# A recurrent scan block: GpSimd's four LayerNorm operations at four steps instead of one

## The chip, the cores and the metric

The kernel runs on one core of a Trainium2 chip. The metric is the device time of one execution in microseconds; lower is better. Engines are named TensorE (PE in the profile), VectorE (DVE), ScalarE (ACT), GpSimd (POOL) and SyncE (SP).

## What is computed

The input has 32 sequences ("rows" below, 0 to 31) of 512 tokens with 256 channels. Per row:

```
xn  = (x - mean(x)) / sqrt(var(x) + 1e-5)            # LayerNorm over the 256 channels
s   = scan_forward(xn) + reverse(scan_backward(reverse(xn)))
g   = silu(xn + 0.3 * expert_ffn(xn))                # one of 8 experts per row, exact GELU inside
out = x + s * g

# each scan, 16 states per channel and direction:
delta, B, C = project(xn);  delta = softplus(delta @ W + b)
h[t] = exp(delta[t] * A) * h[t-1] + delta[t] * B[t] * xn[t]
y[t] = sum over states of C[t] * h[t]  +  D * xn[t]
```

## The kernel before

**Stages.** A prologue prepares weights and row 0. Then every row is a loop over 32 steps `s`, one for each state (16 forward, 16 backward). In a step:
- a decay, exp(delta * A), is made by ScalarE (`make_decay`), two steps ahead or more;
- the input term bx = dx * B is made by GpSimd for 18 of the 32 states (`times_b`, the states in `POOL_B`: 0 to 4, 7, 10, 12, 16 to 21, 23, 25, 27, 31), and for the other 14 by ScalarE (`scale_dx`) and TensorE (transposes);
- VectorE runs the recurrence over the 512 tokens and 2 x 128 channels (`scan`, L868, tile hs);
- hs is multiplied by C, on GpSimd for the 15 states in `POOL_C` (2, 4, 5, 7, 9 to 12, 16, 18, 20, 22, 24, 26, 27), four steps after their own (`C_LAG = 4`), on VectorE for the others (both write hc);
- TensorE sums the hc in PSUM (`add_state`).

Large operations of GpSimd are all 128 x 1024 in float32. Below, "bx 4", "hc 27" and "scan 31" are these operations for states 4, 27 and 31.

**What runs ahead.** While row r is scanned, the "front" of row r + 1 is done in the same 32 steps: tables of step numbers at the top of the kernel say at which step an engine issues which piece. For LayerNorm:
- step 0 (`MEAN`), VectorE: `mean_variance`, after scan 0 of row r: `bn_stats` and `bn_aggr` (L808, L811) give mv;
- step 1 (`SCALE`), ScalarE: `normalise_scale` (L547 to L553): lnv = ln(var + eps), nvar, nmean, rs = exp(-0.5 lnv), rsq = rs squared;
- step 6 (`SHIFT`), GpSimd: `shift_of`, one Newton step on rs: nwt = rsq * nvar, nwt = nwt + 1.5, rs = nwt * rs, shift = nmean * rs, each on 128 x 4 elements and each waiting for the one before;
- step 6 (`NORM`), ScalarE: `normalise` writes xn.

**What sets the order.** Nothing is scheduled by a tool: every engine issues its instructions in the order of the code, and an instruction whose semaphore hasn't been reached holds those behind it on its engine. In a step GpSimd issues, in this order, `times_b`, `times_c`, the rest of this row's front, the next row's front, and `residual` of the row before at step 4 (its og). An lg (`log1p`, second direction of the row being scanned) also stands at step 4.

**Buffers.** bx has 4 slots (`RING`), hs 4 (`HSLOTS`), hc 4. `scan` of state s writes slot s % 4 of hs, and so waits until hc of state s - 4 has been made, by GpSimd's count `s_hcp` where that state is in `POOL_C`:

```python
used = s - HSLOTS
if used % STEPS in POOL_C:
    wait(dve, s_hcp, (row if used >= 0 else row - 1) * NPC + on_pool(used % STEPS) + 1)
```

In ScalarE's loop body of step 31 stand: the decay of state 1 of the next row (it waits for scan 31 of this row), the second copy dxT, SiLU, GELU and the table load behind them; of step 0: the decay of state 2; of step 1: the decay of state 3, `scale_dx` and `normalise_scale`.

Of the kernel before, what the change touches and what calls it, by code (L numbers as in the profile page):

```python
# [5 lines left out]
def mamba_moe_block(nc, x, xw_f, dtw_f, dtb_f, alog_f, d_f, xw_b, dtw_b, dtb_b, alog_b, d_b,  # L6
# [12 lines left out]
    ALU, ACT = mybir.AluOpType, mybir.ActivationFunctionType  # L19
# [4 lines left out]
    C = T // P  # L24
    N = alog_f.shape[1]
    R = dtw_f.shape[1]
    NE, _, F = w1.shape
    FT = F // P
    STEPS = 2 * N
# [4 lines left out]
    BRING, CRING, C_AHEAD = 6, 5, 3  # L34
    TSLOTS, XSLOTS = 3, 3

    MEAN, SCALE, SHIFT, NORM = 0, 1, 6, 6
    TRANS, XNT, PROJECT, HIGH, LOW = (6, 7), (8, 9), (8, 9), 11, 12
    B_TURN, B_COPY = 11, 13
    EXPAND, ABS = (14, 15, 24, 25), (16, 17, 26, 27)  # L40
# [28 lines left out]
    with ctx:  # L69
        def sb(name, shape, dt=f32):  # L70
            return ctx.enter_context(nc.sbuf_tensor(name, shape, dt))
# [4 lines left out]
        def sem(name):  # L76
            return ctx.enter_context(nc.semaphore(name))
# [47 lines left out]
        rs = sb("rs", [P, C])  # L125
        nvar = sb("nvar", [P, C])
        nmean = sb("nmean", [P, C])
        rsq = sb("rsq", [P, C])
        nwt = sb("nwt", [P, C])
        half_eps = sb("half_eps", [P, 1])  # L130
        shift = sb("shift", [P, C])
# [57 lines left out]
        s_bn, s_mv, s_ln, s_rs, s_shift = (sem(n) for n in ("bn_done", "mv_done", "ln_done", "rs_done", "shift_done"))  # L189
        s_xn, s_xnT = sem("xn_done"), sem("xnT_done")  # L190
# [6 lines left out]
        s_sqr = sem("newton_operands")  # L197
        s_nwt, s_xnwt = sem("newton_steps"), sem("router_newton_steps")
# [15 lines left out]
        def wait(eng, s, value):  # L214

            if not isinstance(value, int) or value > 0:
                eng.wait_ge(s, value)  # L217

        def wait_alone(eng, s, value):

            if not isinstance(value, int) or value > 0:
                eng.wait_ge(s, value)
                eng.sem_inc(s_passed, 1)
# [205 lines left out]
        def _(pool):  # L429
# [13 lines left out]
            def step_x(row, par, g):  # L443
                pool.wait_ge(s_delta, row * 2 + g + 1)
                pool.wait_ge(s_xnT, row * 2 + 2)

                wait(pool, s_dxturn, (row - 1) * 2 * DT + g * DT + DT)
                nc.gpsimd.tensor_tensor(dx[:, g, :, :], delta[:, g * (1 + par), :, :], xnT[:, par, :, :], ALU.mult).then_inc(s_dx, 1)  # L448

            def cut(row, par, g):  # L450

                pool.wait_ge(s_dx, row * 2 + g + 1)
                later, edge = (1, 0) if g == 0 else (0, T - 1)
                nc.gpsimd.memset(delta[:, g * (1 + par), later, edge:edge + 1], NO_CARRY).then_inc(s_cut, 1)

            def log1p(row, g):
                pool.wait_ge(s_ratio, row * 2 + g + 1)
                nc.gpsimd.tensor_tensor(lg[:, :, :], lg[:, :, :], ex[:, g, :, :], ALU.mult).then_inc(s_log1p, 1)  # L458

            def step_size(row, par, g):  # L460
                pool.wait_ge(s_log1p, row * 2 + g + 1)
                pool.wait_ge(s_relu, row * 4 + 2 * g + 2)
                nc.gpsimd.tensor_tensor(delta[:, g * (1 + par), :, :], lg[:, :, :], delta[:, g * (1 + par), :, :], ALU.add).then_inc(s_delta, 1)  # L463
# [23 lines left out]
            def residual(row):  # L487
                pool.wait_ge(s_yg, row + 1)
                pool.wait_ge(s_xr, row * 16 + 16)
                nc.gpsimd.tensor_tensor(og[:, :, :], og[:, :, :], xres[:, :, :], ALU.add).then_inc(s_out, 1)  # L490

            def shift_of(row):

                wait_alone(pool, s_sqr, row * 3 + 3)
                wait(pool, s_xn, row * C)
                G = nc.gpsimd
                G.tensor_tensor(nwt[:, :], rsq[:, :], nvar[:, :], ALU.mult).then_inc(s_nwt, 1)
                wait_alone(pool, s_nwt, row * 3 + 1)
                G.tensor_scalar(nwt[:, :], nwt[:, :], 1.5, None, ALU.add).then_inc(s_nwt, 1)
                pool.wait_ge(s_nwt, row * 3 + 2)  # L500
                G.tensor_tensor(rs[:, :], nwt[:, :], rs[:, :], ALU.mult).then_inc(s_nwt, 1)
                pool.wait_ge(s_nwt, row * 3 + 3)
                G.tensor_tensor(shift[:, :], nmean[:, :], rs[:, :], ALU.mult).then_inc(s_shift, 1)

            def front(row, par, s):
                if s == SHIFT:
                    shift_of(row)
                if s in LOG1P:
                    log1p(row, LOG1P.index(s))
                if s in STEPSIZE:  # L510
                    step_size(row, par, STEPSIZE.index(s))
                if s in DX:
                    step_x(row, par, DX.index(s))
                if s in CUT:
                    cut(row, par, CUT.index(s))

            shift_of(0)
            log1p(0, 0)
            step_size(0, 0, 0)
# [3 lines left out]
            def body(row, par, last):  # L523
                for s in range(STEPS):
                    if s in POOL_B:
                        times_b(row, s)
                    if s - C_LAG in POOL_C:
                        times_c(row, s - C_LAG)
                    front(row, par, s + STEPS)
                    if not last:  # L530
                        front(row + 1, 1 - par, s)
                    if s == Y_RESIDUAL and not (isinstance(row, int) and row == 0):
                        residual(row - 1)
# [723 lines left out]
```

## Time and profile before

| | |
|---|---|
| median of 3 runs | 3113.33 us (3111.51 to 3114.2) |
| profiled execution | 3109.25 us |
| its span, first to last instruction | 3107.4 us |
| busy, GpSimd / VectorE / ScalarE / TensorE | 3013.3 / 3021.9 / 2940.2 / 2481.6 us |
| GpSimd's large operations, bx (576) and hc (480) | 1360.9 and 1133.6 us busy |
| VectorE's scans (576 and 448) | 1310.2 and 1005.6 us busy |
| mean granted TensorE clock | 0.961 of full speed |

"Busy" is the time in which an instruction of the engine is under way. The profile gives each instruction's start and duration; on GpSimd and VectorE neighbouring instructions overlap slightly, so the distance from one start to the next tells better what an instruction costs its engine than its duration. Idle time is what passed on an engine between two instructions, and the releaser is the instruction that ended it.

### The profile page before, as it was taken

What the parts mean: (1) busy time and instruction counts of PE and PEld (TensorE: products, weight loads), DVE (VectorE), ACT (ScalarE), POOL (GpSimd) and SP (SyncE); (2) the same over time, 40 slices, a digit from 0 to 9 for tenths busy, and PEclk for the clock granted to TensorE, in tenths of its full rate; (3) what the DMA queues carried; (4) which work ended last, traced back from release to release, by engine and by line L of the source; (5) the groups of instructions that cost most, each with busy time, mean ns of one, the idle gap of its engine ahead of it and who ended that gap; (6) DMA issues with size and microseconds to landing.
All of it is one profiled execution on the core that took longest, in us unless ns stands there. A gap on an engine that the chain in (4) does not pass through costs nothing. (4 is left out here: it accounts for less than half of the span.)

```text
span 3107.4 us, 49213 instructions
## 1 busy us (share of the span) xinstructions
PE 2481.6 (80%) x15990; PEld 1965.3 (63%) x15990; DVE 3021.9 (97%) x1995; ACT 2940.2 (95%) x5242; POOL 3013.3 (97%) x1486
## 2 busy tenths in 40 slices
PE   8788877888878878778888788787788787887886
PEld 6666666666656666666666566666666666666665
DVE  4999999999999999999999999999999999999999
ACT  6899999999999999999999999999999999999995
POOL 3999999999999999999999999999999999999997
PEclk9999999999999999999999999999999999999998
DMA  6443334443334443344443344433444433444341
GB/s 208 121 141 125 125 108 130 141 134 117 122 122 129 143 125 122 114 127 139 134 125 123 113 131 144 128 116 121 122 140 136 125 122 109 131 144 131 108 122 55
DMA packets 258004, 394.17 MB, mean 127 GB/s; under 512 B 45003, under 2 KB 99028, under 8 KB 257748
## 3 DMA queue, kind: packets, MB, share of 16 engines
q1 hardware_dynamic: 257748, 391.03, 41.4%
q8 instruction: 127, 2.08, 0.3%
q14 instruction: 129, 1.06, 0.1%
HBM read 348.98 MB, written 25.18 MB: 120 GB/s over the span
## 5 line engine op out<-in xcount | busy, mean ns | idle before, releaser
L483 POOL TENSOR_TENSOR bx<-dx,b_sb 128x1024 f32<-128x1024 f32 x576 | 1360.9, 2383 | 0.9 <-PE y L1105 0.8
L868 DVE TENSOR_TENSOR_SCAN hs<-decay,bx 128x1024 f32<-128x1024 f32 x576 | 1310.2, 2279 | 15.4 <-POOL bx L483 5.3
L471 POOL TENSOR_TENSOR hc<-hs,c_sb 128x1024 f32<-128x1024 f32 x480 | 1133.6, 2371 | 22.7 <-DVE hs L868 21.0
L1105 PE MATMUL y<-ident,hc 128*128 128x128 f32 x8192 | 1068.3, 277 | 36.2 <-DVE hc L847 36.2
L1105 PEld LDWEIGHTS y<-ident,hc 128*128 128x128 f32 x8192 | 941.9, 143 | 148.7 <-DVE hc L847 106.2
L868 DVE TENSOR_TENSOR_SCAN hs<-decay_sb,decay 128x1024 f32<-128x1024 f32 x448 | 1005.6, 2268 | 11.7 <-issue 10.4
L685 ACT ACTIVATE decay<-delta,rate 128x512 f32<-128x512 f32 x1152 | 745.7, 684 | 41.1 <-DVE hs L868 36.6
L597 ACT ACTIVATE dxb<-dxT,btok 128x256 f32<-128x256 f32 x1792 | 759.2, 503 | 0.4 <-PE decay L1078 0.3
L1078 PE MATMUL decay<-ident,dxb 128*128 128x128 f32 x3584 | 477.2, 276 | 246.0 <-DVE hs L868 212.5
L847 DVE TENSOR_TENSOR hc<-hs,c 128x1024 f32<-128x1024 f32 x544 | 651.0, 1197 | 6.2 <-PE c L1086 5.5
L1078 PEld LDWEIGHTS decay<-ident,dxb 128*128 128x128 f32 x3584 | 396.5, 141 | 402.5 <-issue 258.9
L685 ACT ACTIVATE decay_sb<-delta,rate 128x512 f32<-128x512 f32 x896 | 588.8, 716 | 0.1
L1086 PE MATMUL c<-dbc,selector 128*128 128x512 f32 x544 | 271.3, 499 | 203.0 <-DVE hc L847 203.0
L1047 PE MATMUL front<-w2o_sb,hT 128*128 128x256 f32 x1024 | 297.3, 442 | 39.1 <-issue 39.1
L1031 PE MATMUL front<-xnT,w_sb 128*128 128x512 f32 x512 | 244.3, 599 | 41.6 <-ACT delta L610 41.5
L1047 PEld LDWEIGHTS front<-w2o_sb,hT 128*128 128x128 f32 x1024 | 218.0, 224 | 79.9 <-issue 48.2
L1086 PEld LDWEIGHTS c<-dbc,selector 128*128 128x128 f32 x544 | 105.7, 194 | 256.0 <-DVE hc L847 248.4
L458 POOL TENSOR_TENSOR lg<-lg,ex 128x1024 f32<-128x1024 f32 x64 | 152.0, 2375 | 29.3 <-ACT lg L627 29.0
L1031 PEld LDWEIGHTS front<-xnT,w_sb 128*128 128x128 f32 x512 | 87.3, 190 | 116.8 <-issue 61.2
L463 POOL TENSOR_TENSOR delta<-lg,delta 128x1024 f32<-128x1024 f32 x64 | 152.3, 2380 | 0.1
L448 POOL TENSOR_TENSOR dx<-delta,xnT 128x1024 f32<-128x1024 f32 x64 | 151.7, 2370 | 0.1
L587 ACT ACTIVATE dxT<-front 128x512 f32<-128x512 f32 x128 | 75.1, 587 | 33.6 <-PE front L1007 33.6
(128 smaller groups left out, 2037.6 us busy)
## 6 DMA issues: line engine op xcount, KB each, us to landing
b_sb<-b_scratch SPq DMA_DIRECT2D x576, 256.0 KB, 3.3
c_sb<-b_scratch SPq DMA_DIRECT2D x480, 256.0 KB, 3.6
xin<-in_L_attn_x_dram SPq DMA_DIRECT2D x32, 512.0 KB, 6.3
w_sb<-in_L_ffn_W_dram SPq DMA_DIRECT2D x32, 512.0 KB, 3.4
w2o_sb<-w2o_scratch SPq DMA_DIRECT2D x32, 512.0 KB
xres<-in_L_attn_x_dram SPq DMA_DIRECT2D x32, 512.0 KB, 5.4
out_dram<-og SPq DMA_DIRECT2D x32, 512.0 KB, 4.3
dbc<-high SPq DMA_DIRECT2D x64, 128.0 KB, 2.3
```

The source lines that it names most:

```text
L463: nc.gpsimd.tensor_tensor(delta[:, g * (1 + par), :, :], lg[:, :, :], delta[:, g * (1 + par), :, :], ALU.add).then_inc(s_delta, 1)
L471: nc.gpsimd.tensor_tensor(hc[:, s % RING, :, :], hs[:, s % HSLOTS, :, :], c_sb[:, i % CRING, :].unsqueeze(1).broadcast_to([P, DT, T]), ALU ...
L483: nc.gpsimd.tensor_tensor(bx[:, i % RING, :, :], dx[:, g, :, :], b_sb[:, i % BRING, :].unsqueeze(1).broadcast_to([P, DT, T]), ALU.mult).th ...
L597: A(dxb[:, (row * NT + i) % XSLOTS, c, :], dxT[:, g, c, :], ACT.Copy, scale=btok[:, par, c, g, n:n + 1]).then_inc(s_dxb, 1)
L685: return A(to[:, k, :], delta[:, g * (1 + par), k, :], ACT.Exp, scale=rate[:, g, k, n:n + 1])
L847: V.tensor_tensor(hc[:, s % RING, :, :], hs[:, s % HSLOTS, :, :], cps[:, :].unsqueeze(1).broadcast_to([P, DT, T]), ALU.mult).then_inc(s_hc, 1)
L868: V.tensor_tensor_scan(hs[:, s % HSLOTS, :, :].rearrange("p k t -> p (k t)")[:, u], factor.rearrange("p k t -> p (k t)")[:, u], data.rearr ...
L1031: ins = M(fps[:, :], w1_sb[:, k, j * P:(j + 1) * P], xnT[:, par, k, :], start=(k == 0), stop=(k == DT - 1))
L1047: M(to, hT[:, j, c * P:(c + 1) * P], w2o_sb[:, j, :], start=(j == 0), stop=False)
L1078: ins = nc.tensor.transpose(dps[s % DSLOTS][:, k, c * P:(c + 1) * P], dxb[:, (row * NT + i) % XSLOTS, c, k * P:(k + 1) * P], ident[:, :])
L1086: M(cps[:, :], selector[:, N + n:N + n + 1].broadcast_to([P, P]), dbc[:, par, g, :], start=True, stop=True).then_inc(s_cps, 1)
L1105: ins = M(yps[:, c, k * P:(k + 1) * P], hc[:, s % RING, k, c * P:(c + 1) * P], ident[:, :], start=False, stop=(s == ADDED[-1]), is_transpo ...
```

## The change

GpSimd's `shift_of` is split into four functions. The product is issued at step 3 of the row before, the sum with 1.5 at step 4, the new rs at step 5 and shift at step 6. The product waits for ScalarE's three operands; the wait for the xn of the row before, which protects rs and shift from being overwritten too early, now stands at rs. In the prologue the four are called one behind the other. Nothing else is changed.

```diff
--- before.py
+++ after.py
@@ -34,7 +34,7 @@
     BRING, CRING, C_AHEAD = 6, 5, 3
     TSLOTS, XSLOTS = 3, 3
 
-    MEAN, SCALE, SHIFT, NORM = 0, 1, 6, 6
+    MEAN, SCALE, SHIFT, NORM = 0, 1, (3, 4, 5, 6), 6
     TRANS, XNT, PROJECT, HIGH, LOW = (6, 7), (8, 9), (8, 9), 11, 12
     B_TURN, B_COPY = 11, 13
     EXPAND, ABS = (14, 15, 24, 25), (16, 17, 26, 27)
@@ -489,21 +489,32 @@
                 pool.wait_ge(s_xr, row * 16 + 16)
                 nc.gpsimd.tensor_tensor(og[:, :, :], og[:, :, :], xres[:, :, :], ALU.add).then_inc(s_out, 1)
 
+            def newton_product(row):
+
+                pool.wait_ge(s_sqr, row * 3 + 3)
+                nc.gpsimd.tensor_tensor(nwt[:, :], rsq[:, :], nvar[:, :], ALU.mult).then_inc(s_nwt, 1)
+
+            def newton_sum(row):
+                pool.wait_ge(s_nwt, row * 3 + 1)
+                nc.gpsimd.tensor_scalar(nwt[:, :], nwt[:, :], 1.5, None, ALU.add).then_inc(s_nwt, 1)
+
+            def newton_deviation(row):
+                pool.wait_ge(s_nwt, row * 3 + 2)
+                wait(pool, s_xn, row * C)
+                nc.gpsimd.tensor_tensor(rs[:, :], nwt[:, :], rs[:, :], ALU.mult).then_inc(s_nwt, 1)
+
             def shift_of(row):
-
-                wait_alone(pool, s_sqr, row * 3 + 3)
-                wait(pool, s_xn, row * C)
-                G = nc.gpsimd
-                G.tensor_tensor(nwt[:, :], rsq[:, :], nvar[:, :], ALU.mult).then_inc(s_nwt, 1)
-                wait_alone(pool, s_nwt, row * 3 + 1)
-                G.tensor_scalar(nwt[:, :], nwt[:, :], 1.5, None, ALU.add).then_inc(s_nwt, 1)
-                pool.wait_ge(s_nwt, row * 3 + 2)
-                G.tensor_tensor(rs[:, :], nwt[:, :], rs[:, :], ALU.mult).then_inc(s_nwt, 1)
                 pool.wait_ge(s_nwt, row * 3 + 3)
-                G.tensor_tensor(shift[:, :], nmean[:, :], rs[:, :], ALU.mult).then_inc(s_shift, 1)
+                nc.gpsimd.tensor_tensor(shift[:, :], nmean[:, :], rs[:, :], ALU.mult).then_inc(s_shift, 1)
 
             def front(row, par, s):
-                if s == SHIFT:
+                if s == SHIFT[0]:
+                    newton_product(row)
+                if s == SHIFT[1]:
+                    newton_sum(row)
+                if s == SHIFT[2]:
+                    newton_deviation(row)
+                if s == SHIFT[3]:
                     shift_of(row)
                 if s in LOG1P:
                     log1p(row, LOG1P.index(s))
@@ -514,6 +525,9 @@
                 if s in CUT:
                     cut(row, par, CUT.index(s))
 
+            newton_product(0)
+            newton_sum(0)
+            newton_deviation(0)
             shift_of(0)
             log1p(0, 0)
             step_size(0, 0, 0)
```

GpSimd's queue from step 3 on of any row but the first and last (nwt and rs, shift are the four operations; bx, hc, lg and og are large ones). Before:

```order
L483 TENSOR_TENSOR bx<-dx,b_sb 128x1024 [waits scan_done,b_loaded3]
L483 TENSOR_TENSOR bx<-dx,b_sb 128x1024 [waits scan_done,b_loaded4]
L458 TENSOR_TENSOR lg<-lg,ex 128x1024 [waits ratio_done]
L490 TENSOR_TENSOR og<-og,xres 128x1024 [waits xres_loaded,yg_done]
L471 TENSOR_TENSOR hc<-hs,c_sb 128x1024 [waits sum_states_done,c_loaded0,scan_done]
L497 TENSOR_TENSOR nwt<-rsq,nvar 128x4 [waits newton_operands,xn_done]
L499 TENSOR_SCALAR nwt<-nwt 128x4 [waits newton_steps]
L501 TENSOR_TENSOR rs<-nwt,rs 128x4 [waits newton_steps]
L503 TENSOR_TENSOR shift<-nmean,rs 128x4 [waits newton_steps]
L483 TENSOR_TENSOR bx<-dx,b_sb 128x1024 [waits scan_done,b_loaded5]
```

The same place in the changed kernel:

```order
L483 TENSOR_TENSOR bx<-dx,b_sb 128x1024 [waits scan_done,b_loaded3]
L495 TENSOR_TENSOR nwt<-rsq,nvar 128x4 [waits newton_operands]
L483 TENSOR_TENSOR bx<-dx,b_sb 128x1024 [waits scan_done,b_loaded4]
L458 TENSOR_TENSOR lg<-lg,ex 128x1024 [waits ratio_done]
L499 TENSOR_SCALAR nwt<-nwt 128x4 [waits newton_steps]
L490 TENSOR_TENSOR og<-og,xres 128x1024 [waits xres_loaded,yg_done]
L504 TENSOR_TENSOR rs<-nwt,rs 128x4 [waits xn_done,newton_steps]
L471 TENSOR_TENSOR hc<-hs,c_sb 128x1024 [waits sum_states_done,c_loaded0,scan_done]
L508 TENSOR_TENSOR shift<-nmean,rs 128x4 [waits newton_steps]
L483 TENSOR_TENSOR bx<-dx,b_sb 128x1024 [waits scan_done,b_loaded5]
```

The product, which waits for ScalarE's "newton_operands", was behind bx 4, lg, og and hc 2 and is now ahead of them; the other three stand one large operation apart, and shift has its place ahead of bx 7.

The same steps in row 0, on GpSimd, where there is no og of a row before. Before:

```order
L483 TENSOR_TENSOR bx<-dx,b_sb 128x1024 [waits b_loaded3]
L483 TENSOR_TENSOR bx<-dx,b_sb 128x1024 [waits scan_done,b_loaded4]
L458 TENSOR_TENSOR lg<-lg,ex 128x1024 [waits ratio_done]
L471 TENSOR_TENSOR hc<-hs,c_sb 128x1024 [waits c_loaded0,scan_done]
L497 TENSOR_TENSOR nwt<-rsq,nvar 128x4 [waits newton_operands,xn_done]
L499 TENSOR_SCALAR nwt<-nwt 128x4 [waits newton_steps]
L501 TENSOR_TENSOR rs<-nwt,rs 128x4 [waits newton_steps]
L503 TENSOR_TENSOR shift<-nmean,rs 128x4 [waits newton_steps]
L483 TENSOR_TENSOR bx<-dx,b_sb 128x1024 [waits scan_done,b_loaded5]
```

and in the changed kernel:

```order
L483 TENSOR_TENSOR bx<-dx,b_sb 128x1024 [waits b_loaded3]
L495 TENSOR_TENSOR nwt<-rsq,nvar 128x4 [waits newton_operands]
L483 TENSOR_TENSOR bx<-dx,b_sb 128x1024 [waits scan_done,b_loaded4]
L458 TENSOR_TENSOR lg<-lg,ex 128x1024 [waits ratio_done]
L499 TENSOR_SCALAR nwt<-nwt 128x4 [waits newton_steps]
L504 TENSOR_TENSOR rs<-nwt,rs 128x4 [waits xn_done,newton_steps]
L471 TENSOR_TENSOR hc<-hs,c_sb 128x1024 [waits c_loaded0,scan_done]
L508 TENSOR_TENSOR shift<-nmean,rs 128x4 [waits newton_steps]
L483 TENSOR_TENSOR bx<-dx,b_sb 128x1024 [waits scan_done,b_loaded5]
```

Here the product moved ahead of bx 4, lg and hc 2. No instruction moved on another engine.

## Rows read from the trace of the kernel before

**Rows 1.** The page, part 1: busy us (share of the span) x instructions
```profile
PE 2481.6 (80%) x15990; PEld 1965.3 (63%) x15990; DVE 3021.9 (97%) x1995; ACT 2940.2 (95%) x5242; POOL 3013.3 (97%) x1486
```

**Rows 2.** Lines, GpSimd, whole span: out<-in xcount | busy us, mean ns | idle before
```profile
L497 POOL TENSOR_TENSOR nwt<-rsq,nvar 128x4 f32<-128x4 f32 x32 | 6.6, 206 | 11.2 <-ACT rsq L553 11.2
```

**Rows 3.** Timeline, GpSimd, row 12: start us, us, instruction, [idle before <-releaser]
```profile
1200.10 11.66 POOL L483 TENSOR_TENSOR bx<-dx,b_sb 128x1024 f32<-128x1024 f32 x5
1211.73 2.35 POOL L458 TENSOR_TENSOR lg<-lg,ex 128x1024 f32<-128x1024 f32 x1
...
1218.68 0.20 POOL L497 TENSOR_TENSOR nwt<-rsq,nvar 128x4 f32<-128x4 f32 x1
1219.07 0.22 POOL L499 TENSOR_SCALAR nwt<-nwt 128x4 f32<-128x4 f32 x1 [0.20 <-POOL nwt L497]
...
1219.65 0.20 POOL L503 TENSOR_TENSOR shift<-nmean,rs 128x4 f32<-128x4 f32 x1
1219.81 2.38 POOL L483 TENSOR_TENSOR bx<-dx,b_sb 128x1024 f32<-128x1024 f32 x1
```

**Rows 4.** Timeline, ScalarE, row 12
```profile
1203.43 1.30 ACT L685 ACTIVATE decay<-delta,rate 128x512 f32<-128x512 f32 x2 [0.18 <-DVE hs L868]
1204.68 0.58 ACT L587 ACTIVATE dxT<-front 128x512 f32<-128x512 f32 x1
...
1216.91 0.20 ACT L553 ACTIVATE rsq<-rs 128x4 f32<-128x4 f32 x1
...
1228.56 2.06 ACT L560 ACTIVATE xn<-xin,shift,rs 128x256 f32<-128x256 f32 x4
```

**Rows 5.** Timeline, VectorE, start of row 12
```profile
1201.06 2.28 DVE L868 TENSOR_TENSOR_SCAN hs<-decay,bx 128x1024 f32<-128x1024 f32 x1
...
1204.37 2.28 DVE L868 TENSOR_TENSOR_SCAN hs<-decay,bx 128x1024 f32<-128x1024 f32 x1
...
1209.22 0.38 DVE L811 BATCH_NORM_AGGREGATE mv<-stats 128x2 f32<-128x6 f32 x4
```

**Rows 6.** Timeline, GpSimd, end of row 12 (hc 24, hc 27, next bx 0)
```profile
1282.74 2.35 POOL L471 TENSOR_TENSOR hc<-hs,c_sb 128x1024 f32<-128x1024 f32 x1
...
1292.26 2.38 POOL L471 TENSOR_TENSOR hc<-hs,c_sb 128x1024 f32<-128x1024 f32 x1
1294.61 2.37 POOL L483 TENSOR_TENSOR bx<-dx,b_sb 128x1024 f32<-128x1024 f32 x1
```

**Rows 7.** Timeline, VectorE, end of row 12 (scans 28 and 29, 31, 0)
```profile
1286.65 4.44 DVE L868 TENSOR_TENSOR_SCAN hs<-decay_sb,decay 128x1024 f32<-128x1024 f32 x2
...
1295.43 2.28 DVE L868 TENSOR_TENSOR_SCAN hs<-decay,bx 128x1024 f32<-128x1024 f32 x1
...
1298.74 2.28 DVE L868 TENSOR_TENSOR_SCAN hs<-decay,bx 128x1024 f32<-128x1024 f32 x1
```

**Rows 8.** Timeline, GpSimd, row 0
```profile
44.99 11.64 POOL L483 TENSOR_TENSOR bx<-dx,b_sb 128x1024 f32<-128x1024 f32 x5
...
73.09 0.20 POOL L497 TENSOR_TENSOR nwt<-rsq,nvar 128x4 f32<-128x4 f32 x1 [5.96 <-ACT rsq L553]
```

**Rows 9.** Timeline, ScalarE, row 0
```profile
72.71 0.21 ACT L553 ACTIVATE rsq<-rs 128x4 f32<-128x4 f32 x1
```

**Rows 10.** Timeline, VectorE: scan 4 of row 0, scan 0 of rows 1 and 31
```profile
74.19 2.29 DVE L868 TENSOR_TENSOR_SCAN hs<-decay,bx 128x1024 f32<-128x1024 f32 x1 [0.56 <-issue]
...
161.40 2.29 DVE L868 TENSOR_TENSOR_SCAN hs<-decay,bx 128x1024 f32<-128x1024 f32 x1
...
3004.39 2.29 DVE L868 TENSOR_TENSOR_SCAN hs<-decay,bx 128x1024 f32<-128x1024 f32 x1
```

**Rows 11.** Windows: us; busy us of each engine; PEclk, DMA share, GB/s
```profile
1210.00:1216.00 6.00, 5.06 (x16) 3.63 (x17) 6.00 (x4) 5.97 (x10) 6.00 (x3) 0.57 0.56 175
```

**Rows 12.** Timeline, TensorE, before ScalarE's copy at 1204.68
```profile
1201.54 1.91 PE L1105 MATMUL y<-ident,hc 128*128 128x128 f32 x16
1203.28 0.60 PE L1007 MATMUL front<-ident,dx 128*128 128x128 f32 x4
```

## The prediction

> **What bounds the kernel now.** I read the page first: GpSimd is busy 97% of the span, VectorE 97%, ScalarE 95% [rows 1]. With three engines so full, whichever waits loses, so I read one row in the timelines (row 12; "S" is the start of its scan of state 0, 1204.37 [rows 5]). GpSimd: its large operations start every 2.32 us, back to back; the only place without one is the Newton chain, which holds the engine from 1218.68 to the start of the next bx at 1219.81, 1.13 us for four operations of 0.2 us [rows 3]. VectorE: from this S to the next, 1298.74, are 94.37 us [rows 7]. The mean over rows 1 to 31 is (3004.39 - 161.40) / 30 = 94.77 us [rows 10]. GpSimd and VectorE thus run in step, about evenly full.
>
> Next I asked where the chain's input comes from. Its first product needs rsq, the fifth of ScalarE's small activations. ScalarE waits 0.18 us for VectorE's scan of state 31 (started 1201.06 [rows 5], the wait stands at 1203.43 [rows 4]) and from there works through its queue: two decays, a copy, SiLU and GELU with their table loads, four decays, four scalings, then the small ones for LayerNorm up to rsq, which ends at 1216.91 + 0.20 = 1217.11 [rows 4]. The statistics themselves were there at 1209.22 + 0.38 = 1209.60 [rows 5]: what is late is ScalarE's turn, not the data. So rsq is ready 16.05 us after the start of scan 31, or S + 12.74. Today the product starts at 1218.68, 1.57 us later, and over all 32 rows it waited only 11.2 us, mostly in the first two [rows 2].
>
> **The change, part by part.**
>
> *Product moved from step 6 to step 3.* On GpSimd it now stands ahead of bx of state 4. Five bx take from 1200.10 to the lg at 1211.73, so bx 4 starts at 1211.73 - 2.32 = 1209.41 [rows 3]. The product would stand there, and its input comes at 1217.11: a wait of 7.7 us. GpSimd works in order, so bx 4, lg, og, hc, bx 7 and all that follows wait too. Nothing covers this: GpSimd has no spare time [rows 1]. The question is only how much of it comes back through slack.
>
> *The three others* find their inputs done (each follows its predecessor by a large operation). Apart, each costs what lies between the start of shift and the next start, 19.81 - 19.65 = 0.16 us [rows 3]. Bounds: 0.05 and 0.3 us (0.3 is the spacing inside the chain; below, an operation hidden by its large neighbours). I take 0.16, the same kind of operation beside the same kind. Four cost 0.64 instead of 1.13: 0.5 us saved per row, range 0 to 1.
>
> *How much slack is there?* If GpSimd falls behind VectorE, who waits first? VectorE's scan of state s overwrites the hs slot of state s - 4 and so waits for GpSimd's hc of it. hc of state 27 ends at 1292.26 + 2.38 = 1294.64 [rows 6], scan 31 starts 1295.43 [rows 7]: 0.79 us of slack. hc 24 ends 1285.09, scan 28 starts 1286.65: 1.56. The next row's bx 0 ends at 1294.61 + 2.37 = 1296.98, its scan 0 starts 1298.74: 1.76 [rows 6, 7]. A wait of 7.7 us cannot be stored in 0.79, and it is not paid once either: ScalarE is released by scan 31, so when scan 31 waits for GpSimd, rsq is later by the same amount. That closes a loop, and its length is the new period of a row:
> - start of scan 31 to end of rsq: 16.05 [rows 4, 5]
> - release of the product by rsq: in the first row rsq ends at 72.92 and the product starts at 73.09 after waiting: 0.17 [rows 8, 9]
> - product 0.16; bx 4, lg, og, hc: 1218.68 - 1209.41 = 9.27; the other three small ones 3 x 0.16 = 0.48 [rows 3]
> - from bx 7 (1219.81) to the end of hc 27 (1294.64), unchanged work: 74.83 [rows 3, 6]
> - release of scan 31: 0.04 (nothing shows it for this pair; between 0.02 and the 0.18 of ScalarE's wait above).
>
> Sum 101.00 us, against 94.77: +6.23 per row. This is the wait of 7.7 less the 0.5 saved and the 0.79 of slack, roughly. There are 30 such periods (rows 1 to 30; row 31 has no next row to normalise, and its 103 us to the end stay as they are). 30 x 6.23 = 187 us.
>
> *First row.* Its bx 3 ends at about 54.3 (five bx from 44.99), and the product waits until 73.09 for the rsq it waits for already [rows 8]. bx 4 then ends at 73.25 + 2.36 = 75.6, and scan 4, which started at 74.19, needs it [rows 10]: +1.4 us. Beyond that GpSimd waits for VectorE in this row anyway.
>
> *Prologue, SP queue, PE.* In the prologue the four calls keep their order and nothing lies between them: 0. GpSimd issues no DMA; the SP queue's loads of b and c wait for GpSimd's counts and move with it, several loads ahead: 0. ScalarE's normalising of xn needs shift. With the terms above shift starts at 12.74 + 0.17 + 0.16 + 9.27 + 0.32 = S + 22.66 and ends 0.2 later; xn starts at 1228.56, S + 24.19 [rows 4]: 0. PE's additions of GpSimd's hc come later, but the scans and their own hc, which PE adds too, come later by nearly as much: 0, with the 1 us that eight additions take (16 in 1.91 [rows 12]) as the upper bound per row.
>
> **Sum.** 187 + 1.4 = 188. The profiled execution took 3109.25 us (span 3107.40): 3109.25 + 188 = 3297.6. The median of the runs stands 4.1 us above that execution, so 3301. With the bounds (small operations 0.4 to 0.5 us either way per row, releases 0.2, PE up to 1 us more) the case itself reaches from 3280 to 3335.
>
> **A rule that says the opposite.** In the rows, GpSimd and VectorE are both at 97% [rows 1] and the product's wait decides. The Trainium skill, "Perfetto Trace Analysis", section "Identifying the Most-Contended Engine", says to take the engine with the highest occupancy as the bound and to optimise it first. By that rule the sum would be the saving alone. That rule's case is the first rival below.
>
> **Rivals.**
> 1. *Faster: the wait doesn't happen, or happens once.* GpSimd loses only the chain's latency: 31 x 0.5 = 15 us, 3098. It needs rsq before GpSimd is through with bx 3, 7.7 us earlier than today against GpSimd. It decides at 0.5 us: a shorter wait than that is a gain. Against it: ScalarE's unbroken queue from scan 31 to rsq, and only 0.79 us of slack at scan 31. The Trainium skill's rule of the most-contended engine points to this time. Chance 0.02; a balance near zero 0.02 more.
> 2. *Slower, but less.* If scan 31 isn't what holds VectorE but scan 0 is (bx 0 ends 2.34 us after hc 27, while scan 0 starts 3.31 us after scan 31), up to 0.97 us per row is not paid, and ScalarE gains as much on its queue while VectorE waits: up to 2 us per row, 3241 to 3272. Against: hs has four slots and the code's wait names hc 27. Chance 0.06.
> 3. *Slower still.* ScalarE's stretch gets longer. It holds a copy that PE feeds, and PE's granted clock is not always full: 0.57 of 1.00 between 1210 and 1216, so the lower of its two levels (1.2 and 2.4 GHz) for most of it [rows 11]. If PE, now more idle, gets it elsewhere, the 16 additions (1.9 us) and 4 transposes (0.6) ahead of this copy take twice their time, less the 0.8 us between the transposes' end and the copy [rows 4, 12]: 1.7 us more per row, with what stands ahead of them about 2: 3361. Chance 0.10.
>
> **How the numbers follow.** The forecast case has 0.80, predicted time 3301. The range takes it whole and the nearer parts of rivals 2 and 3: 3262 to 3345. Within 0.2% (6 us) is what a measurement of this kernel can't tell from no change. Faster 0.02, same 0.02, slower 0.96.
>
> **What the new profile should show.** GpSimd's product with some 7 us of idle time ahead of it in each of 31 rows, released by rsq, in all near 210 to 240 us with the first row's 18.6; GpSimd's busy share down to about 91%. Rows of one length, 101.0 us. VectorE waiting for GpSimd at scans 28 and 31 and, before them, in the first half of the row, together 6.6 us per row. rsq still 16.05 us after the start of scan 31. I am wrong if the product's idle time is small, or if it is 7 us and the rows are nevertheless shorter than 99 us.

## The result, and the profile after

| | before | changed |
|---|---|---|
| median | 3113.76 us (4 runs) | 3304.11 us (4 runs, 3300.68 to 3304.54) |
| ratio, 95% interval | | 1.0611 [1.0599, 1.0624] |
| profiled execution / its span | 3109.25 / 3107.40 us | 3300.68 / 3298.9 us |
| mean length of rows 1 to 30 | 94.77 us | 101.13 us |
| mean granted TensorE clock | 0.961 | 0.917 |

The changed kernel is 190 us (6.1%) slower. The forecast was 3301 us in a range of 3262 to 3345.

The page of the changed kernel, span and part 1 (compare [rows 1]):

```profile
span 3298.9 us, 49180 instructions
...
PE 2612.7 (79%) x15990; PEld 2087.3 (63%) x15990; DVE 3042.6 (92%) x1995; ACT 2942.0 (89%) x5242; POOL 3008.7 (91%) x1486
```

All engines do the same work in a longer time. GpSimd's busy time is even 5 us less, though its share falls from 97% to 91%. The line of the product (columns as in [rows 2]) has the difference:

```profile
L495 POOL TENSOR_TENSOR nwt<-rsq,nvar 128x4 f32<-128x4 f32 x32 | 6.5, 203 | 238.0 <-ACT rsq L567 238.0
```

238.0 us of idle time stand ahead of the 32 products, against 11.2 before. 5.2 of the 238.0 us are the prologue's, in both kernels. The idle time ahead of GpSimd's hc, nearly all of it for VectorE, fell from 22.7 to 3.5 us meanwhile.

One row, row 12 again. GpSimd's timeline (compare [rows 3]):

```profile
1270.75 9.35 POOL L483 TENSOR_TENSOR bx<-dx,b_sb 128x1024 f32<-128x1024 f32 x4
1287.06 0.20 POOL L495 TENSOR_TENSOR nwt<-rsq,nvar 128x4 f32<-128x4 f32 x1 [6.96 <-ACT rsq L567]
1287.21 2.38 POOL L483 TENSOR_TENSOR bx<-dx,b_sb 128x1024 f32<-128x1024 f32 x1
1289.53 2.39 POOL L458 TENSOR_TENSOR lg<-lg,ex 128x1024 f32<-128x1024 f32 x1
1291.86 0.24 POOL L499 TENSOR_SCALAR nwt<-nwt 128x4 f32<-128x4 f32 x1
1292.05 2.39 POOL L490 TENSOR_TENSOR og<-og,xres 128x1024 f32<-128x1024 f32 x1
1294.38 0.22 POOL L504 TENSOR_TENSOR rs<-nwt,rs 128x4 f32<-128x4 f32 x1
1294.53 2.37 POOL L471 TENSOR_TENSOR hc<-hs,c_sb 128x1024 f32<-128x1024 f32 x1
1296.85 0.21 POOL L508 TENSOR_TENSOR shift<-nmean,rs 128x4 f32<-128x4 f32 x1
1297.01 2.38 POOL L483 TENSOR_TENSOR bx<-dx,b_sb 128x1024 f32<-128x1024 f32 x1
```

Four bx end at 1280.10, the product starts at 1287.06: 6.96 us of idle time, ended by rsq. Behind it everything is as dense as before. The other three find their inputs ready; from the start of shift to the next bx are 0.16 us, as before, and for the others it is 0.15 us (0.19 for the sum with 1.5): from product to bx 7 are 9.95 us, four large operations and four small ones.

ScalarE (compare [rows 4]) and VectorE at the start of the same row (compare [rows 5]; scan 31, then scan 0):

```profile
1273.30 1.30 ACT L699 ACTIVATE decay<-delta,rate 128x512 f32<-128x512 f32 x2 [0.55 <-DVE hs L882]
...
1286.78 0.21 ACT L567 ACTIVATE rsq<-rs 128x4 f32<-128x4 f32 x1
...
1300.00 2.08 ACT L574 ACTIVATE xn<-xin,shift,rs 128x256 f32<-128x256 f32 x4 [1.16 <-DVE zz L836]
```

```profile
1270.92 2.29 DVE L882 TENSOR_TENSOR_SCAN hs<-decay,bx 128x1024 f32<-128x1024 f32 x1 [0.63 <-POOL hc L471]
...
1274.24 2.28 DVE L882 TENSOR_TENSOR_SCAN hs<-decay,bx 128x1024 f32<-128x1024 f32 x1
```

rsq ends at 1286.99, 16.07 us after the start of scan 31 (1270.92); before, these were 16.05. And scan 31 itself now has idle time ahead of it, 0.63 us, ended by a GpSimd hc.

The end of the row, GpSimd's hc 24 and hc 27 (compare [rows 6]) and VectorE's scans 28, 31 and 0 (compare [rows 7]):

```profile
1359.86 2.40 POOL L471 TENSOR_TENSOR hc<-hs,c_sb 128x1024 f32<-128x1024 f32 x1
...
1369.46 2.36 POOL L471 TENSOR_TENSOR hc<-hs,c_sb 128x1024 f32<-128x1024 f32 x1
```

```profile
1362.40 4.46 DVE L882 TENSOR_TENSOR_SCAN hs<-decay_sb,decay 128x1024 f32<-128x1024 f32 x2 [1.25 <-ACT decay_sb L699]
...
1371.95 2.29 DVE L882 TENSOR_TENSOR_SCAN hs<-decay,bx 128x1024 f32<-128x1024 f32 x1 [0.66 <-POOL hc L471]
...
1375.27 2.28 DVE L882 TENSOR_TENSOR_SCAN hs<-decay,bx 128x1024 f32<-128x1024 f32 x1
```

hc 27 ends at 1371.82, scan 31 starts at 1371.95: the 0.79 us of slack are gone, and the loop is closed. Scan 28 waited 1.25 us; the profile names a decay of ScalarE as the last releaser, but by ScalarE's timeline this decay had been done some 12 us earlier, and hc 24 ended at 1359.86 + 2.40 = 1362.26, 0.14 us ahead of the scan. That is one of the cases in which the named releaser isn't the one that held. VectorE's own list of waits shows the sums that carry GpSimd's name (us in total, times, longest):

```profile
DVE hs L882 <- POOL hc L471: 117.0, 128, 1.9
DVE hs L882 <- POOL bx L483: 48.0, 32, 5.3
```

### The profile page after: what moved, and what is told of

Read it like the earlier page. It is cut to its first block, busy times and chain, and to the rows that moved or that the text cites. A ratio compares the mean times of both kernels' runs of the same rounds, so it can differ in the third digit from the quotient of the medians.

```text
span 3298.9 us, 49180 instructions
## 1 busy us (share of the span) xinstructions
PE 2612.7 (79%) x15990; PEld 2087.3 (63%) x15990; DVE 3042.6 (92%) x1995; ACT 2942.0 (89%) x5242; POOL 3008.7 (91%) x1486
## 4 chain that ended last, share of the span: by engine, by line
POOL 24%; PE 18%; issue 13%; ACT 11%; DVE 7%; DMA 1%; POOLq 0%; DVEq 0%; ACTq 0%; SPq 0%
POOL hc L471 10%; POOL bx L483 9%; PE y L1119 6%; PE front L1061 4%; DVE hs L882 4%; ACT decay L699 4%; ACT dxb L611 3%; DVE hc L861 3%; POOL delta L463 2%; PE decay L1092 2%; PE c L1100 2%; POOL dx L448 2%; ACT decay_sb L699 1%; PE y L1109 1%; POOL lg L458 1%
## 5 line engine op out<-in xcount | busy, mean ns | idle before, releaser
L1119 PE MATMUL y<-ident,hc 128*128 128x128 f32 x8192 | 1151.4, 291 | 84.0 <-POOL hc L471 43.3
L1119 PEld LDWEIGHTS y<-ident,hc 128*128 128x128 f32 x8192 | 1009.0, 150 | 213.1 <-DVE hc L861 104.9
L1092 PE MATMUL decay<-ident,dxb 128*128 128x128 f32 x3584 | 506.2, 287 | 300.7 <-DVE hs L882 241.2
L1092 PEld LDWEIGHTS decay<-ident,dxb 128*128 128x128 f32 x3584 | 422.5, 148 | 457.6 <-issue 269.7
L1100 PE MATMUL c<-dbc,selector 128*128 128x512 f32 x544 | 285.1, 524 | 162.2 <-DVE hc L861 162.2
L1100 PEld LDWEIGHTS c<-dbc,selector 128*128 128x128 f32 x544 | 112.4, 207 | 199.7 <-DVE hc L861 192.3
L495 POOL TENSOR_TENSOR nwt<-rsq,nvar 128x4 f32<-128x4 f32 x32 | 6.5, 203 | 238.0 <-ACT rsq L567 238.0
```

The source lines that it names most:

```text
L1092: ins = nc.tensor.transpose(dps[s % DSLOTS][:, k, c * P:(c + 1) * P], dxb[:, (row * NT + i) % XSLOTS, c, k * P:(k + 1) * P], ident[:, :])
L1100: M(cps[:, :], selector[:, N + n:N + n + 1].broadcast_to([P, P]), dbc[:, par, g, :], start=True, stop=True).then_inc(s_cps, 1)
L1119: ins = M(yps[:, c, k * P:(k + 1) * P], hc[:, s % RING, k, c * P:(c + 1) * P], ident[:, :], start=False, stop=(s == ADDED[-1]), is_transpo ...
```

## The experiments

The theory: a row's length is that of a closed loop, scan 31, ScalarE's queue up to rsq, the product's wait, GpSimd's work to hc 27, and scan 31 again. The rivals: small operations cost something by standing apart (1.5 us each would do); or the bound is another and the wait only goes along. In the arithmetic of the expectations, 3113 and 3304 are the medians of the two kernels. Every run's ratio is to the kernel before, run on the same chip.

**Where the product stands.** Three runs with the product alone at step 3, 4 and 5, the other three a chain at step 6:

```diff
-    MEAN, SCALE, SHIFT, NORM = 0, 1, (3, 4, 5, 6), 6
+    MEAN, SCALE, SHIFT, NORM = 0, 1, (3, 6, 6, 6), 6      # first run; then (4, 6, 6, 6) and (5, 6, 6, 6)
```

> Only the product stands at step 3; sum, rs and shift are a chain at step 6 again. Theory (the product's wait for rsq is all of it; the period of a row is the loop through that wait): the loop keeps its wait and pays 0.73 us for a chain of three in place of 3 x 0.16: 101.1 + 0.25 us per row, 3304 + 8 = 3312. Rival (the cost comes from small operations standing apart among large ones, 190 us over 4 x 31 operations, about 1.5 us each): only one of four stands apart, 3113 + 48 = 3161.

> Product at step 4 (behind bx 4 and lg, ahead of og), the other three a chain at step 6. Theory: two large operations (4.64 us) leave the part of the loop that lies behind the wait: 16.06 + 0.08 + 0.16 + 4.64 + 0.73 + 74.83 + 0.13 = 96.6 us per row against 94.77: 3113 + 56 = 3169, and the product waits some 2.5 us per row. Rival (cost per operation that stands apart): as with the product at step 3, 3161, and the wait doesn't set the time; by it this run and the one before are equal.

> Product at step 5 (behind og, ahead of hc 2), the other three a chain at step 6. Theory: the loop is 16.06 + 0.08 + 0.16 + 2.32 + 0.73 + 74.83 + 0.13 = 94.3 us, below the 94.4 to 94.8 that VectorE needs for a row, so it no longer sets the time although the product still waits (some 0.5 us or less per row): 3106 to 3120, no change that can be told. Rival (cost per operation apart): 3161.

Measured: 3309.29 us (1.063 [1.0612, 1.0648]), 3172.38 us (1.0191 [1.0174, 1.0208]) and 3112.78 us (1.000 [0.9991, 1.001]). The product's line in the three:

```profile
L495 POOL TENSOR_TENSOR nwt<-rsq,nvar 128x4 f32<-128x4 f32 x32 | 6.4, 201 | 236.8 <-ACT rsq L567 236.8
```

```profile
L495 POOL TENSOR_TENSOR nwt<-rsq,nvar 128x4 f32<-128x4 f32 x32 | 6.5, 203 | 95.3 <-ACT rsq L567 95.3
```

```profile
L495 POOL TENSOR_TENSOR nwt<-rsq,nvar 128x4 f32<-128x4 f32 x32 | 6.5, 203 | 33.0 <-ACT rsq L567 32.3
```

The rival is out: with one operation apart the loss is not a quarter but all of it and 5 us more, and it shrinks by 137 us when the same operation stands two large ones later. The theory's 3312, 3169 and 3106 to 3120 were met within 3.4 us. The third run says most about reading: there the product still waits, 33.0 us in all (5.2 in the prologue, 14.0 in the first row, 0.0 to 1.4 in each of the others), and the kernel isn't slower. The loop is only about 94.3 us long with this product, and what the product waits is what VectorE's row was longer than that: 0.01 us after a row of 94.38 us, 0.47 after one of 94.79, 0.85 after one of 95.16. From row 1 on, hc 27 still ends at least 0.15 us ahead of scan 31, so nothing of it reaches VectorE. In that kernel's row 12 the product stands directly between two large operations (GpSimd's timeline):

```profile
1219.48 0.20 POOL L495 TENSOR_TENSOR nwt<-rsq,nvar 128x4 f32<-128x4 f32 x1
1219.63 2.36 POOL L471 TENSOR_TENSOR hc<-hs,c_sb 128x1024 f32<-128x1024 f32 x1
1221.95 0.23 POOL L499 TENSOR_SCALAR nwt<-nwt 128x4 f32<-128x4 f32 x1
```

**The four places without the wait.**

```diff
-                pool.wait_ge(s_sqr, row * 3 + 3)
-                nc.gpsimd.tensor_tensor(nwt[:, :], rsq[:, :], nvar[:, :], ALU.mult).then_inc(s_nwt, 1)
+                if isinstance(row, int) and row == 0:
+                    pool.wait_ge(s_sqr, 3)
+                nc.gpsimd.tensor_tensor(nwt[:, :], ident[:, 0:C], ident[:, C:2 * C], ALU.mult).then_inc(s_nwt, 1)
...
-                nc.gpsimd.tensor_tensor(rs[:, :], nwt[:, :], rs[:, :], ALU.mult).then_inc(s_nwt, 1)
+                nc.gpsimd.tensor_tensor(rs2[:, :], nwt[:, :], ident[:, 0:C], ALU.mult).then_inc(s_nwt, 1)
...
-                nc.gpsimd.tensor_tensor(shift[:, :], nmean[:, :], rs[:, :], ALU.mult).then_inc(s_shift, 1)
+                nc.gpsimd.tensor_tensor(shift[:, :], ident[:, 0:C], rs2[:, :], ALU.mult).then_inc(s_shift, 1)
```

(The wait for ScalarE is left only in the prologue. And, since shift no longer follows ScalarE's operands, VectorE's `mean_variance` waits for these operands by their own count.)

> The four operations stand at steps 3, 4, 5 and 6 as in the changed kernel, but read only constants, so that none waits for ScalarE. Left out: the Newton step on rs, and shift has nothing to do with the mean (the sizes and counts of operations are the same). Theory (it is the wait alone): the loss is gone, 3098 to 3115. Rival (places or number of gaps cost by themselves): 3304 stays in large part, above 3200.

Measured: 3111.6 us, 0.9997 [0.9987, 1.0006]. The same four places, the same count and size of operations, no loss. Where they stand costs nothing; what the first of them waits for costs everything.

**Whose lateness it is.** The changed kernel with ScalarE's small operations one step earlier in its queue:

```diff
-    MEAN, SCALE, SHIFT, NORM = 0, 1, (3, 4, 5, 6), 6
+    MEAN, SCALE, SHIFT, NORM = 0, 0, (3, 4, 5, 6), 6
```

> The changed kernel with ScalarE's normalise_scale at step 0 in place of 1, that is ahead of one decay pair (1.25 us) and one group of four scalings (1.6 us). Theory (rsq is late because of ScalarE's turn, not its data): rsq comes 2.8 us sooner after the start of scan 31, the loop is 2.8 us shorter, 98.3 us per row: 3304 - 85 = 3219. Rival (rsq is bound by the statistics, or GpSimd's wait is with something else that comes at the same time): 3304 stays.

Measured: 3219.62 us, 1.0343 [1.0328, 1.0359]. The product's line:

```profile
L495 POOL TENSOR_TENSOR nwt<-rsq,nvar 128x4 f32<-128x4 f32 x32 | 6.4, 201 | 152.1 <-ACT rsq L567 152.1
```

The stall fell by 86 us and the time by 84. The statistics are made at the same place of VectorE's queue as before, so it was ScalarE's turn that was late, as [rows 4, 5] had it.

**Where GpSimd's lateness passes on.** The changed kernel with a fifth slot of hs, so that scan 31 waits for hc 26 and no longer for hc 27; for the room, b_sb has five slots instead of six, and a control has the latter alone:

```diff
-    HSLOTS = 4
-    BRING, CRING, C_AHEAD = 6, 5, 3
+    HSLOTS = 5
+    BRING, CRING, C_AHEAD = 5, 5, 3
```

(and the slot is `(row * STEPS + s) % HSLOTS`.)

> The changed kernel with five slots of hs in place of four, and five of b_sb in place of six for the room; the next run is its control. Scan 31 then waits for hc 26, done one large pair earlier, and bx 0 and scan 0 close the loop. Theory (scan 31's wait for hc 27 is the place where GpSimd's lateness passes to VectorE and from there to ScalarE): the loop loses 3.31 - 2.34 - 0.1, some 0.9 to 1.0 us, and up to 1.2 more where ScalarE gets ahead while VectorE waits at scan 0: 3238 to 3276. Rival (hs slots don't matter, the loop closes at scan 0 anyway): as the control.

> Control of the run before: the changed kernel with five slots of b_sb and four of hs. Theory: b arrives early enough either way, 3304. Rival (one slot less makes GpSimd wait for b): above 3315.

Measured: the control 3302.8 us, 1.0617 [1.0599, 1.0634], as the changed kernel; with five slots of hs 3278.53 us, 1.0537 [1.052, 1.0555]. 24 us less than the control: the direction and the place are as expected, the size is 2.5 us short of the range. VectorE now waits for bx, and its list of waits no longer names an hc of GpSimd (of the changed kernel's waits above, some 70% were for hc):

```profile
DVE hs L882 <- POOL bx L483: 131.0, 104, 6.2
```

Most rows are 99.8 us long, 1.2 less than the changed kernel's 101.0. But 5 of the 30 are 101.1 to 101.5. Ahead of such a row, this is ScalarE's queue behind scan 31 (which starts at 860.59), and TensorE's timeline ahead of the second copy:

```profile
862.97 1.30 ACT L699 ACTIVATE decay<-delta,rate 128x512 f32<-128x512 f32 x2 [0.28 <-DVE hs L882]
867.02 0.60 ACT L601 ACTIVATE dxT<-front 128x512 f32<-128x512 f32 x1 [2.74 <-PE front L1021]
```

```profile
862.92 3.31 PE L1119 MATMUL y<-ident,hc 128*128 128x128 f32 x15 [1.80 <-POOL hc L471]
```

TensorE adds the states in order. Its additions waited 1.80 us for GpSimd's hc 27, the transposes that feed ScalarE's second copy stood behind them, the copy had 2.74 us of idle time ahead of it, and rsq came 18.9 us after scan 31 in place of 16.07. But the wait for hc 27 alone doesn't make a row long. Behind the scan 31 at 2463.26 hc 27 is as late, and the additions wait nearly as long:

```profile
2465.58 1.97 PE L1119 MATMUL y<-ident,hc 128*128 128x128 f32 x16 [1.68 <-POOL hc L471]
```

There the copy waits 1.07 us, rsq comes 17.2 us after scan 31, and the next row is 99.7 us long. What sets the long rows apart is how long the 16 additions take: 3.52 us for all of them in the row above and 2.95 to 3.52 us in the five, against 1.97. The granted clock differs as much (windows in the two rows, columns as in [rows 11]):

```profile
863.00:866.00 3.00, 3.00 (x15) 3.00 (x16) 1.75 (x2) 1.27 (x2) 3.00 (x2) 0.52 0.03 10
2465.60:2467.50 1.90, 1.90 (x18) 1.90 (x19) 1.06 (x1) 1.30 (x2) 1.90 (x1) 1.00 0.09 26
```

In all five it is 0.52 to 0.63 during these additions, near the lower level. So two things together make ScalarE's stretch up to 2.9 us longer and undo VectorE's early scan 31: the additions start late, behind hc 27, and they run at the lower clock. The second is the third rival of the prediction. Without these five rows, which cost about 1.6 us each, the run would lie within the range; why the clock is lower there and not elsewhere isn't shown.

**Can the spreading be of use at all?** If the four stand apart where all inputs are there, GpSimd saves what the prediction counted. Two ways of placing them, and as a bound the kernel before without the Newton step:

```diff
-    MEAN, SCALE, SHIFT, NORM = 0, 1, (3, 4, 5, 6), 6
+    MEAN, SCALE, SHIFT, NORM = 0, 0, (5, 6, 7, 8), 6      # all apart; the other: 0, 1, (6, 6, 7, 8), 6
```

```diff
-                G.tensor_tensor(nwt[:, :], rsq[:, :], nvar[:, :], ALU.mult).then_inc(s_nwt, 1)
...
-                G.tensor_tensor(rs[:, :], nwt[:, :], rs[:, :], ALU.mult).then_inc(s_nwt, 1)
-                pool.wait_ge(s_nwt, row * 3 + 3)
```

> normalise_scale at step 0 and the four operations apart at steps 5, 6, 7 and 8, where every input is there in time. GpSimd saves about 0.5 us per row and waits for nothing. Theory (VectorE's own work, 94.4 us, sets the row once GpSimd doesn't wait): no change from before, 3106 to 3114. Rival (GpSimd sets it too, its saving comes through): 31 x 0.5 = 15 us, 3098.

> Product and sum at step 6, rs at 7, shift at 8, normalise_scale where it was. GpSimd saves about 0.3 us per row; no operation waits for ScalarE, and shift (about S + 22.7) is there before ScalarE's xn (S + 24.2). Theory: as before, 3106 to 3116. Rival (GpSimd sets the row): 3104; if shift came too late for xn, some tenths of a us more per row, 3120 to 3130.

> The kernel before with the three Newton operations left out: GpSimd makes only shift = nmean * rs from ScalarE's rs at step 6. Left out: the refinement of rs. GpSimd has 0.98 us less work per row, the most that any placing of these operations could save. Theory (VectorE sets the row): 3104 to 3114. Rival (GpSimd sets it): 31 x 0.98 = 30 us, 3083.

Measured: 3113.41 us (1.0002 [0.9993, 1.0011]), 3112.31 us (0.9999 [0.999, 1.0008]) and 3110.48 us (0.9994 [0.9985, 1.0003]). None differs from the kernel before, not even the last, from which 1 us of GpSimd's work per row was taken. In the first two, GpSimd's saving went into slack: from row 1 on, hc 27 ends at least 1.2 us ahead of scan 31, where before it was 0.5 us at the least. The page of the last:

```profile
span 3109.3 us, 49085 instructions
...
PE 2483.4 (80%) x15990; PEld 1966.9 (63%) x15990; DVE 3021.5 (97%) x1995; ACT 2940.9 (95%) x5242; POOL 2997.4 (96%) x1390
```

GpSimd's busy time is 16 us less than in [rows 1], VectorE's is the same within 1 us and the span within 2. About half of its rows are 94.37 to 94.39 us long, as in the kernel before: that is VectorE's own work. In row 12, one of these, VectorE is idle for only 0.60 us, none of which the profile puts down to another engine.

And the other way, more work on GpSimd in the kernel before, ahead of the chain (an operation of 128 x 256 in the first run, 128 x 512 in the second):

```diff
+                pool.wait_ge(s_extra, row + 1)
+                G.tensor_tensor(extra[:, :], extra[:, :], extra[:, :], ALU.mult).then_inc(s_extra, 1)
```

> The kernel before with one more GpSimd operation of 128x256 (about 0.58 us by the 2.32 us of 128x1024) ahead of the Newton chain in every row: how far is GpSimd from being the bound? Its own row, without waits, is about 94.4 us of back-to-back starts; with 0.58 it is 95.0, VectorE's mean row is 94.77. Theory (the longer of the two sets the row): +0.2 us x 31, 3113 + 7 = 3120. Rival (GpSimd has real spare time): 3113 stays. Rival (both add up): 3113 + 18 = 3131.

> The same with 128x512, about 1.16 us: GpSimd's row is 95.6 us. Theory: (95.6 - 94.77) x 31 = 26 us, 3139. Rival (spare time): 3113 stays. Rival (both add up): 3113 + 36 = 3149.

Measured: 3123.14 us (1.0035 [1.0021, 1.0049]) and 3135.72 us (1.0076 [1.0059, 1.0093]). With the larger one, nearly all rows are about 95.5 us long and VectorE waits for hc. The extra operation's line, and VectorE's largest wait:

```profile
L501 POOL TENSOR_TENSOR extra<-extra 128x512 f32<-128x512 f32 x32 | 33.7, 1052 | 10.8 <-ACT rsq L558 10.8
```

```profile
DVE hs L873 <- POOL hc L474: 22.0, 44, 1.0
```

The extra operation takes 1.0 us from start to start (1231.78 to 1232.78 in row 12), and 95.5 less 1.0 are 94.5: GpSimd's own row, to a tenth VectorE's 94.4. So the two engines' own rows are about equally long, and VectorE's has waits for TensorE on top (mean 94.77). Taking work from GpSimd alone gives nothing, and of 1.0 us more per row 0.77 reach the time ((3135.72 - 3111.97) / 31). The time came out between the theory and a plain sum in the first run (expected 3120) and 3 us below the theory in the second, where the added operation was expected to take 1.16 us and took 1.0.

## Why the prediction was right

- *The stall.* Forecast: some 7 us in each of 31 rows, 210 to 240 us in all, GpSimd busy 91%. Measured: 6.96 us in most rows, 238.0 us with the prologue's 5.2, 91%.
- *The loop.* Its terms in row 12 of the changed kernel, forecast and measured: scan 31 to rsq 16.05 and 16.07; release of the product 0.17 and 0.07; product to bx 7 9.91 and 9.95; bx 7 to the end of hc 27 74.83 and 74.81; release of scan 31 0.04 and 0.13. Sum 101.00 and 101.03. The two releases were off by 0.1 us each, in opposite directions: 0.17 was read in a row in which the product had two semaphores to wait for and now has one; whether that explains it wasn't tried.
- *Rows of one length.* Nearly: 22 of the 30 are 100.96 to 101.06 us, 8 are 101.36 to 101.62, and the mean is 101.13. In seven of these eight, rsq comes 16.4 to 16.7 us after scan 31. One is the row ahead of which scan 31 started at 967.4. ScalarE's timeline, and the window with the granted clock (columns as in [rows 11]):

```profile
965.76 1.30 ACT L699 ACTIVATE decay<-delta,rate 128x512 f32<-128x512 f32 x2 [0.93 <-DVE hs L882]
968.62 0.60 ACT L601 ACTIVATE dxT<-front 128x512 f32<-128x512 f32 x1 [1.56 <-PE front L1021]
```

```profile
964.00:970.00 6.00, 6.00 (x30) 5.70 (x29) 5.36 (x4) 3.51 (x5) 6.00 (x4) 0.54 0.12 44
```

  The first of the two copies waited 1.56 us for TensorE, whose granted clock was 0.54 there, near the lower of its levels (1.2 and 2.4 GHz). In all seven the 16 additions ahead of this copy took 3.62 us and the copy waited 1.56; in the rows with rsq on time they took 1.91 to 3.46 us and it waited 0.85 at most. That is the forecast's third rival on a small scale, at the first copy and not at the second that it named: 0.13 us per row in the mean, 4 us of the 190, not the 2 us per row that it was priced at.
- *The slack.* Scans 28 and 31 wait in all rows from 1 to 30, on average 1.01 and 0.66 us, and the earlier ones (6, 8, 12) 3.9 together. VectorE's idle time ahead of all scans, whatever the profile names as its end, adds up to 6.3 us per row (forecast 6.6; in the kernel before it is 0.5).
- *The first row.* Forecast +1.4 us for the time, and here the prediction was wrong. Its cause is as forecast: GpSimd's product waited 18.68 us and scan 4 came late, at 76.01 in place of 74.19 [rows 10].

```profile
73.44 0.20 POOL L495 TENSOR_TENSOR nwt<-rsq,nvar 128x4 f32<-128x4 f32 x1 [18.68 <-ACT rsq L567]
```

```profile
47.83 2.29 DVE L882 TENSOR_TENSOR_SCAN hs<-decay,bx 128x1024 f32<-128x1024 f32 x1 [5.29 <-POOL bx L483]
...
76.01 2.29 DVE L882 TENSOR_TENSOR_SCAN hs<-decay,bx 128x1024 f32<-128x1024 f32 x1 [1.94 <-POOL bx L483]
...
107.78 4.47 DVE L882 TENSOR_TENSOR_SCAN hs<-decay_sb,decay 128x1024 f32<-128x1024 f32 x2 [0.36 <-issue]
...
161.85 2.28 DVE L882 TENSOR_TENSOR_SCAN hs<-decay,bx 128x1024 f32<-128x1024 f32 x1
...
3195.85 2.28 DVE L882 TENSOR_TENSOR_SCAN hs<-decay,bx 128x1024 f32<-128x1024 f32 x1
```

  The first and the third of these lines (scans 0 and 13 of row 0) in the kernel before:

```profile
47.38 2.29 DVE L868 TENSOR_TENSOR_SCAN hs<-decay,bx 128x1024 f32<-128x1024 f32 x1 [5.28 <-POOL bx L483]
...
107.33 4.46 DVE L868 TENSOR_TENSOR_SCAN hs<-decay_sb,decay 128x1024 f32<-128x1024 f32 x2 [0.59 <-ACT decay_sb L685]
```

  Scan 0 of row 0 already starts 0.45 us later, so the product made scan 4 later by 76.01 - 74.19 - 0.45 = 1.37 us, as forecast. By scan 13 only the 0.45 are left: the row has other waits, and they took up all of the 1.37. From scan 0 of row 0 to scan 0 of row 1 are 114.02 us in both kernels. The term should have been 0. The 0.45 us come from ahead of the first row; in the traces of this case scan 0 of row 0 starts anywhere from 47.4 to 51.0 us, and whether the change has a part in it isn't shown.
- *The sum.* Scan 0 of row 31 starts at 3195.85, so the mean row is (3195.85 - 161.85) / 30 = 101.13. 30 x (101.13 - 94.77) + 0.45 = 191.3; the spans differ by 3298.9 - 3107.4 = 191.5. Forecast 188: the first row's 1.4 too much, and some 4 for the seven rows with the slow additions left out. That these two miss in opposite directions is luck, a small one beside the 187 of the loop.
- *The rivals.* The first one, with 3098 us, took GpSimd as the engine that sets the time. The Trainium skill, "Perfetto Trace Analysis", section "Identifying the Most-Contended Engine", calls the engine with the highest occupancy the most contended one and says to optimise it first. Read strictly, that is VectorE here (3021.9 us busy against GpSimd's 3013.3), and not GpSimd as the prediction had it; the runs without the wait agree with the strict reading, since GpSimd's saving isn't seen in them. Neither reading has the wait in it, which made the kernel 6% slower while GpSimd's busy time fell by 5 us. The second rival, that scan 0 and not scan 31 closes the loop, fell with the timeline above (0.13 us between hc 27 and scan 31, 1.1 us between bx 0 and scan 0) and with the fifth slot of hs.
- *What I had not said.* The prediction took the 0.5 us that GpSimd saves per row as a gain in every case without the wait (first rival, 3098). The runs without the wait show that this gain would not have come: 3111.6. Nor is a wait below 0.5 us a gain, as that rival had it: with the product at step 5 it waits about that long per row, and the time is 3112.78. Counting it was right inside the loop, where GpSimd's time counts, and wrong in the rival.

## What to carry to other kernels

Before an operation is moved ahead in an in-order queue, look up when its input is ready there, not only whether it is ready where it stands: here it was 1.6 us early at the old place and 7.7 us late at the new one, and what made it late was the turn of the operation in its producer's queue. The price of such a wait is found by following the loop that it closes, term by term, and not by its length less some slack; and of several engines at 97%, find out by adding and taking work which of them has any to give before counting a saving.

## What I had not expected of the hardware

- A small operation (128 x 4) between large ones costs GpSimd 0.15 to 0.16 us from start to start (0.19 for the sum with 1.5), while its recorded duration is 0.20 to 0.24 us; in the chain, each waiting for the one before, 0.28 to 0.39 us.
- TensorE, with the same work in a longer row, was granted less of its clock (0.917 against 0.961), and its 8192 additions took 291 ns each instead of 277; of this only about 4 us reached the time, in the rows in which the additions ahead of ScalarE's first copy ran at the lower clock throughout.
